# Layer 1's routed experts: the last tile of inner features, features 640 to 703 before, begins at feature 576 and spans 128

## The reference, cut to what matters

```python
def _L1_ffn_ref(x, gate_w, gate_b, w1, b1, w3, b3, w2, b2, sw1, sb1, sw3, sb3, sw2, sb2):
    ...
    scores = jax.nn.softmax(logits.astype(jnp.float32), axis=-1)
    top_vals, top_idx = jax.lax.top_k(scores, TOPK)
    ...
    h = jnp.einsum('td,edh->teh', xf, w1) + b1
    g = jnp.einsum('td,edh->teh', xf, w3) + b3
    a = jax.nn.silu(h) * g
    y = jnp.einsum('teh,ehd,te->td', a, w2, cw) + cw @ b2
    z = jax.nn.silu(xf @ sw1 + sb1) * (xf @ sw3 + sb3) @ sw2 + sb2
    return (y + z).reshape(shape)
```

## Time and profile before

| | us |
|---|---|
| median of 3 runs | 2023.27 (2022.45 to 2024.18) |
| the profiled execution, its own time | 2018.79 |
| its span, first to last instruction | 2017.1 |
| PE busy | 1900.9 (94%) |
| DVE busy | 691.0 (34%) |
| ACT busy | 561.0 (28%) |
| POOL busy | 201.3 (10%) |
| PE, weight loads | 1293.5 (64%) |

### The profile page before, as it was taken

How to read it: one execution, slowest core, us unless ns; L and a number is a source line. 1 busy time by engine, 2 the same in 40 slices (tenths; PEclk the granted TensorE clock), 3 DMA queues, 4 the chain that set the end, 5 groups by cost and what they waited for, 6 DMA issues and landing times.

```text
span 2017.1 us, 26698 instructions
## 1 busy us (share of the span) xinstructions
PE 1900.9 (94%) x10722; PEld 1293.5 (64%) x10722; DVE 691.0 (34%) x1706; ACT 561.0 (28%) x1263; POOL 201.3 (10%) x293
## 2 busy tenths in 40 slices
PE   5999999999999999998999978999898999999995
PEld 3677777777548447555777755777545544777773
DVE  4234344343335654421000145555425322111111
ACT  2333333332123224212222235444425200111110
POOL 0000000000010232322111031111001110000001
PEclk9999999999999998999999998999899999999998
DMA  5011111101320010027999730102212300877762
GB/s 194 22 42 43 37 69 43 42 22 64 125 104 1 21 42 30 36 83 259 352 354 352 277 119 32 48 32 90 105 42 84 149 22 16 318 289 285 284 252 80
DMA packets 43802, 245.19 MB, mean 122 GB/s; under 512 B 5929, under 2 KB 6433, under 8 KB 20880
## 3 DMA queue, kind: packets, MB, share of 16 engines
q1 hardware_dynamic: 30752, 213.22, 28.7%
q0 software_dynamic: 6000, 17.58, 2.7%
q10 hardware_dynamic: 6912, 12.52, 1.6%
HBM read 227.73 MB, written 15.57 MB: 121 GB/s over the span
## 4 chain that ended last, share of the span: by engine, by line
PE 86%; DVE 5%; issue 5%; DMA 2%; POOL 1%; ACT 1%; POOLq 0%; SPq 0%; DVEq 0%; ACTq 0%
PE bank L224 25%; PE bank L548 25%; PE bank L1606 10%; PE bank L230 8%; PE bank L690 3%; PE bank L718 2%; PE bank L2483 2%; PE bank L637 2%; PE bank L644 2%; PE bank L1186 2%; PE bank L1590 1%; PE bank L983 1%; PE bank L997 1%; PE bank L1211 1%; PE bank L975 1%
## 5 line engine op out<-in xcount | busy, mean ns | idle before, releaser
L548 PE MATMUL bank<-split 128*128 128x512 f32 x2208 | 549.1, 401 | 24.9 <-DVE split L521 12.3
L548 PEld LDWEIGHTS bank<-split 128*128 128x128 f32 x2208 | 407.3, 190 | 155.6 <-issue 31.6
L224 PEld LDWEIGHTS bank<-arena,weights 128*128 128x128 f32 x1984 | 229.7, 187 | 36.1 <-issue 33.7
L224 PE MATMUL bank<-xnT,weights 128*128 128x512 f32 (+1 forms) x592 | 246.7, 577 | 4.7 <-DVE xnT L880 3.1
L224 PE MATMUL bank<-arena,weights 128*128 128x128 f32 (+1 forms) x1984 | 245.1, 282 | 2.8 <-DVE arena L1597 1.8
L224 PEld LDWEIGHTS bank<-xnT,weights 128*128 128x128 f32 x592 | 113.2, 193 | 132.1 <-issue 124.8
L1606 PE MATMUL bank<-weights,arena 128*128 128x512 f32 (+1 forms) x368 | 166.6, 596 | 0.0
L230 PE MATMUL bank<-weights,arena 128*128 128x512 f32 x288 | 131.9, 611 | 8.3 <-ACT arena L2366 6.0
L1606 PEld LDWEIGHTS bank<-weights,arena 128*128 128x128 f32 (+1 forms) x368 | 65.9, 190 | 72.6 <-issue 72.6
L2593 DVE SCALAR_TENSOR_TENSOR arena<-bank,cols,arena 128x128 f32<-128x128 f32 x96 | 28.8, 345 | 230.7 <-PE bank L224 227.9
L230 PEld LDWEIGHTS bank<-weights,arena 128*128 128x128 f32 x288 | 54.8, 196 | 73.3 <-issue 62.9
(11 more groups left out here) (284 smaller groups left out, 2014.5 us busy)
## 6 DMA issues: line engine op xcount, KB each, us to landing
weights<-in_L_ffn_re_w SPq DMA_DIRECT2D x62, 1024.0 KB, 8.2
weights<-in_L_w SPq DMA_DIRECT2D x20, 1408.0 KB, 12.0
arena<-in_ctxT SPq DMA_DIRECT2D x24, 1024.0 KB, 5.0
arena<-in_L_w SPq DMA_DIRECT2D x12, 1408.0 KB, 7.6
weights<-in_L_w_full SPq DMA_DIRECT2D x10, 1280.0 KB, 9.5
expert_out<-arena ACTq DMA_DIRECT2D x47, 256.0 KB, 8.3
weights<-in_L_ffn_sw SPq DMA_DIRECT2D x9, 1024.0 KB, 5.0
arena<-in_L_w_full SPq DMA_DIRECT2D x6, 1280.0 KB, 9.8
```

Source lines behind the costliest of these rows:

```text
L224: s = pe.matmul(out, w[:, k, j0:j0 + m], rhs(k), start=(k == 0), stop=(k == KT - 1))
L548: s = pe.matmul(bank[:, :], still, moving, start=(n == 0), stop=(n == len(order) - 1))
```

## The change

The last of layer 1's six tiles takes features 576 to 703, that is 128 of them, instead of 640 to 703. Its first 64 features are those of the tile before it once more. They are kept out of the result: ACT and DVE compute only partitions 64 to 127 of that tile, and partitions 0 to 63 of it in the three `hid` buffers are set to zero once, by three memsets on DVE after the fence, for which PE waits (`hid_zero`). The part of `w2` for the last tile is 128 rows in memory instead of 64, and the bias columns are laid out to match on the host.

```diff
-LAST1 = INTER1 - (HT1 - 1) * P
+LAST1 = INTER1 - P
...
-            self.rows_of = [P] * (hidden_tiles - 1) + [last_rows]
+            self.first_of = [m * P for m in range(hidden_tiles - 1)] + [last_first]
+            self.own_of = [0] * (hidden_tiles - 1) + [(hidden_tiles - 1) * P - last_first]
...
-                r = self.rows_of[m]
-                s = pe.matmul(banks[6 + ex % 2][:, :], self.hid[ex % 2][0:r, m, :], w2.view[0:r, m, :], start=(m == 0),
+                s = pe.matmul(banks[6 + ex % 2][:, :], self.hid[ex % 2][:, m, :], w2.view[:, m, :], start=(m == 0),
...
-            sp.dma_start(buf[0:LAST1, full:full + DIM], A["L1_w2_last"][ex]).then_inc(landed, 16)
+            sp.dma_start(buf[:, full:full + DIM], A["L1_w2_last"][ex]).then_inc(landed, 16)
...
         stage_end(pe, "tensor")
+        pe.wait_ge(hid_zero, 3)
         moe1.turn_rows(pe, 0)
...
-                        r, o = moe1.rows_of[m], (m - m0) * P
-                        s = project_into(pe, banks[2 + 2 * n + j][0:r, o:o + P], w.view, m * P, r,
+                        o = (m - m0) * P
+                        s = project_into(pe, banks[2 + 2 * n + j][:, o:o + P], w.view, moe1.first_of[m], P,
...
         stage_end(dve, "vector")
+        for h in (*moe1.hid, moe1.hid_long):
+            dve.memset(h[0:moe1.own_of[HT1 - 1], HT1 - 1, :], 0.0).then_inc(hid_zero, 1)
         moe1.rows_vector(dve, 0)
...
-                dve.scalar_tensor_tensor(out=moe1.hid[ex % 2][0:r, m, :], in0=banks[3 + 2 * n][0:r, o:o + P],
-                                         scalar=col("b3", HT1 * ex + m, 1, 0, r),
-                                         in1=expert_silu[(HT1 * ex + m) % 3][0:r, 0:P], op0=ALU.add,
+                dve.scalar_tensor_tensor(out=moe1.hid[ex % 2][r:P, m, :], in0=banks[3 + 2 * n][r:P, o:o + P],
+                                         scalar=col("b3", HT1 * ex + m, 1, r, P),
+                                         in1=expert_silu[(HT1 * ex + m) % 3][r:P, 0:P], op0=ALU.add,
...
-    A["L1_w2_last"] = w[:, full:]
+    A["L1_w2_last"] = w[:, LAST1:]
```

More of the change, by code:

```diff
@@ L1361, in build_program, with __init__ @@
     class Experts:
-        def __init__(self, layer, n, chosen, hidden_tiles, last_rows, L, S, before=None):
+        def __init__(self, layer, n, chosen, hidden_tiles, last_first, L, S, before=None):
             self.layer, self.n, self.chosen, self.ht = layer, n, chosen, hidden_tiles
-            self.rows_of = [P] * (hidden_tiles - 1) + [last_rows]
+            self.first_of = [m * P for m in range(hidden_tiles - 1)] + [last_first]
+            self.own_of = [0] * (hidden_tiles - 1) + [(hidden_tiles - 1) * P - last_first]
             self.aff, self.top = S(NT, n), S(NT, 8)
@@ L1762, in rest_tensor @@
                     for n, w in enumerate(up):
[L1763 removed]
+                        s = project_into(pe, banks[2 + n][:, 0:3 * P], w, self.first_of[m], P, lambda k: self.tokT_long[:, k, :])
                     s.then_inc(r["mm"], 1)
@@ L1771, in rest_tensor @@
                     for m in range(self.ht):
-                        rows_ = self.rows_of[m]
-                        s = pe.matmul(banks[6][:, :], self.hid_long[0:rows_, m, c * P:(c + 1) * P], w2[0:rows_, m, :],
+                        s = pe.matmul(banks[6][:, :], self.hid_long[:, m, c * P:(c + 1) * P], w2[:, m, :],
                                       start=(m == 0), stop=(m == self.ht - 1))
@@ L1835, in build_program @@
     L(NT, DIM)
-    moe0 = Experts(0, E0, TOP0, HT0, P, L, small_layout())
+    moe0 = Experts(0, E0, TOP0, HT0, (HT0 - 1) * P, L, small_layout())
     sh_hid = Layout(L.at)(KT, TOK)
@@ L2406, in build_program @@
     sh1_mm, sh1_a, sh1_v, sh1_pool = sh_mm.then(22), sh_a.then(11), sh_v.then(11), sh_pool.then(NT)
-    sh1_down, sh1_add = sem("sh1_down"), sem("sh1_add")
+    sh1_down, sh1_add, hid_zero = sem("sh1_down"), sem("sh1_add"), sem("hid_zero")
     GROUPS = [[0, 1, 2, 3], [4, 5, 6, 7], [8, 9, 10]]
@@ L2587, in experts1_vector @@
                 n, j = divmod(m, 4)
-                r, o = moe1.rows_of[m], j * P
+                r, o = moe1.own_of[m], j * P
                 moe1.wait(dve, "silu", HT1 * ex + m + 1)
@@ L2600, in rest_hidden @@
         def rest_hidden(e, ex, m):
-            r = moe1.rows_of[m]
+            r = moe1.own_of[m]
             e.wait_ge(moe1.r["a"], moe1.hidden_a(ex, m))
-            return e.scalar_tensor_tensor(out=moe1.hid_long[0:r, m, :], in0=banks[3][0:r, 0:3 * P],
-                                          scalar=col("b3", HT1 * ex + m, 1, 0, r), in1=expert_silu[0][0:r, :],
+            return e.scalar_tensor_tensor(out=moe1.hid_long[r:P, m, :], in0=banks[3][r:P, 0:3 * P],
+                                          scalar=col("b3", HT1 * ex + m, 1, r, P), in1=expert_silu[0][r:P, :],
                                           op0=ALU.add, op1=ALU.mult)
@@ L2624, in experts1_scalar @@
                 n, j = divmod(m, 4)
-                r, o, at = moe1.rows_of[m], j * P, HT1 * ex + m
+                r, o, at = moe1.own_of[m], j * P, HT1 * ex + m
                 moe1.wait(act, "up_mm", 4 * ex + 2 * n + 1)
@@ L2628, in experts1_scalar @@
                     moe1.wait(act, "hid", at - 2)
-                act.activation(expert_silu[at % 3][0:r, 0:P], banks[2 + 2 * n][0:r, o:o + P], ACT.Silu,
-                               bias=col("b1", at, 1, 0, r)).then_inc(moe1.raised("silu"), 1)
+                act.activation(expert_silu[at % 3][r:P, 0:P], banks[2 + 2 * n][r:P, o:o + P], ACT.Silu,
+                               bias=col("b1", at, 1, r, P)).then_inc(moe1.raised("silu"), 1)
             if ex:
@@ L2640, in rest_silu @@
                 moe1.wait_hidden(e, ex - 1, HT1 - 1)
-            return e.activation(expert_silu[0][0:r, :], banks[2][0:r, 0:3 * P], ACT.Silu,
-                                bias=col("b1", HT1 * ex + m, 1, 0, r))
+            return e.activation(expert_silu[0][r:P, :], banks[2][r:P, 0:3 * P], ACT.Silu,
+                                bias=col("b1", HT1 * ex + m, 1, r, P))
         moe1.if_over(act, lambda e: moe1.rest_scalar(e, rest_silu))
@@ L2746, in column, with overlapped @@
         return v.reshape(-1, P).T
+    def overlapped(v):
+        return np.concatenate([v[:, 0:(HT1 - 1) * P], v[:, LAST1:]], 1)
     def rope_half(w, half):
@@ L2791, in lay_out @@
         "bq": column(I["L1_xattn_bq"]), "bk": column(I["L1_xattn_bk"]), "bv": column(I["L1_xattn_bv"]),
-        "b1": column(padded(I["L1_ffn_b1"], HT1 * P).reshape(-1)),
-        "b3": column(padded(I["L1_ffn_b3"], HT1 * P).reshape(-1)),
+        "b1": column(overlapped(I["L1_ffn_b1"]).reshape(-1)), "b3": column(overlapped(I["L1_ffn_b3"]).reshape(-1)),
         "sb1": column(I["L1_ffn_sb1"]), "sb3": column(I["L1_ffn_sb3"])}
```

1 line of the change is left out of this document (removed).

## The result

| | before | after |
|---|---|---|
| median | 2023.34 us (8 runs, 2019.14 to 2024.18) | 2008.31 us (8 runs, 2005.80 to 2015.10) |
| ratio, 95% interval | | 0.9932 (0.9918 to 0.9945) |
| the profiled execution's span | 2017.1 us | 2006.8 us |

The kernel is faster by 15.0 us in the medians. The ratio, 0.9932, by itself is 13.8 us, and its interval makes it 11 to 17 us.

A forecast was written before the change was run, and what follows sets the result against it. PE's own stream was taken as the bound. Savings of 12.9 + 0.9 + 0.7 + 1.2 = 15.7 us, less 1.0 for memsets and wait, take 14.7 off the 2023.27 median: 2008.6 us, range 2004 to 2013.

The forecast's parts named there:

- PE's stream alone sets the stage: Layer 1's expert stage: a microsecond taken from PE's stream comes off the end, one added on other engines is hidden.
- Removed, a period: Per expert in layer 1, priced by layer 0: 17.29 us becomes 16.30, 0.99 less; 13 periods give 12.9 us.
- The ends: Last period without transposes 16.80 to 15.87 us, 0.93 less; two final down projections 11.15 to 10.48, 0.67 less.
- Memsets and the wait: Behind the fence, three DVE memsets delay PE's first transpose by 1.0 us, bounds 0.4 to 1.4; a gain is excluded.
- Costed at nothing, ACT and DVE on other partitions: Last tile's 64x128 instructions move to other partitions at no cost, with over 190 us of waiting for PE as cover.
- Costed at nothing, the larger w2: w2's last part is 256 KB instead of 128, 4.87 MB an expert, hidden by about 11 us of cover.
- The sum: 15.7 us saved on PE less 1.0 for memsets and wait: 14.7 us less for the whole kernel.
- Run level: Profiled execution 2018.79 us becomes 2004.1; timed runs lie 4.5 higher, so the median 2023.27 becomes 2008.6.
- wide loads in line: Rival, layer 1 up projections: 256 wider weight loads at 56 ns give back 14.3 us, no gain, 2022.9 us; 3%.
- the partial removal: Rival: stalls at transposes and down-to-up borders stay, about 0.35 us a period; gain some 10 us, 2014; 3%.
- the DMA bound: Rival: 274 GB/s is all the stage can draw, 17.8 us an expert, slower at 2027.7 us; 2%.
- The rival of one half-clock piece more or less: PE after the fence: one half-clock stretch more gives 2010.2 us, one less 2007.0; 10% for one more.

The follow-up runs named there:

- both halves: The changed kernel with only the down projection wide, 2018.25 us (ratio 0.9981 to before), and with only the up projections wide, 2013.37 us (0.9961).
- narrow_grouped: The kernel before with its last four up tiles reordered so the two narrow ones stand together, same matmuls; 2016.24 us, ratio 0.9979.
- layer0_rows64: The changed kernel with 64 rows instead of 128 in the last inner tile of layer 0's down projections; 2019.03 us, ratio 0.9990 to the kernel before.
- zero_rows_w2: The changed kernel without memsets or PE's wait; ACT and DVE compute all 128 partitions, w2's doubled rows are zeros; 2005.06 us, again 2005.57.

## Why the prediction was right

Its forecast was 2008.6 us for a median of 2008.31. By its steps:

- **PE's stream alone sets the stage.** Right: in the steady stretch PE is busy for 211.00 of 211.00 us after as before, and both halves shortened the end by what they took from the stream.
- **Removed, a period.** Forecast 16.30 us; measured 16.306. Up 10.72 (10.71 forecast), transposes 0.43 (0.43), down 5.15 (5.16). Pricing by layer 0's identical code needed no theory of the stall at all. That it is the crossing, and not the narrow matmul or its load, was only argued then; `narrow_grouped` and `layer0_rows64` show it.
- **The ends.** The last period 15.87 (15.87), the last two down projections 10.47 (10.48).
- **Memsets and the wait.** Forecast 1.0 us, measured 0.90: three memsets in 0.71 us, not 0.95, and 0.19 until the first of them starts. The prediction excluded a gain; there is a small one, 1.51 us in place of 1.61 from the first transposes to the up projections behind them, so the net cost was 0.8. Why is open.
- **Costed at nothing, ACT and DVE on other partitions.** This step failed for one expert. 190 us of idle time hide it in general, but at expert 1 there is no down projection behind the transposes, and PE waits for DVE's copy. There up starts 1.92 us behind the transposes in place of 1.49 (1729.51 to 1731.00), 0.43 later. 0.09 of it are there in `zero_rows_w2` too (1.58): DVE's first product starts 0.27 us behind the transposes with all tiles wide, 0.18 before. Of the other 0.34, the upper partitions make up about 0.24 and the three memsets the rest. The cover was an average over the stage, while the prediction itself says that experts 0 and 1 have no down projection ahead of them.
- **Costed at nothing, the larger w2.** Right: PE waited for no weight.
- **The sum.** From the last `x_tok` addition to the end 15.9 us less, of which 1.6 are the clock of the first expert, leaves 14.3; forecast 14.7, less the 0.43 missed, and 0.2 back from the memsets, is 14.5. The forecast's parts hold one by one to within 0.2 us.
- **Run level.** That the changed kernel's profiled execution would be 2004.1 us was wrong by 4.4 (its own time 2008.53): the two profiled executions do not share a clock history. The step on the median, which took only the difference, held. That 2008.6 met 2008.31 this closely is partly chance, as the interval of 11 to 17 us says.

Of the rivals, wide loads in line fell by the period, the partial removal by the border from down to up (12 starts of down in 5.15 us are 0.43 each, the step into up included), the DMA bound by 300 GB/s at a share of 0.78, with PE busy throughout. The rival of one half-clock piece more or less did show in single executions, both ways: the first expert's up projections took 10.79 us in one execution of the changed kernel and 12.14 in another.

## What to carry to other kernels

Where most stationary operands fill the array and a few take only half its rows or columns, look at the distances between matmul starts on both sides of the few: here a crossing pair cost 0.3 to 0.4 us. The half tile saves next to nothing against that, since the moving operand is as wide as ever: the widened matmuls start 0.112 us apart in the changed kernel, and eight narrow ones, crossing included, took 1.02 us. Fill the tile up, by overlap with zeros in the weight, or at least put the narrow tiles side by side. A stage of the same kernel that runs the same code without the odd shape gives the price better than any model. And a cost is hidden only where its cover stands: check the first and the last iteration of a software pipeline on their own.

## What the runs showed of the hardware that I had not expected

- 96 rows or 96 columns cost no crossing (periods 7.45 and 7.43 us against 7.44), 64 of either do (7.84 and 7.72). So do 31 rows (3.62 us for eight matmuls in place of 3.44), but transposes with 16 stationary columns don't (0.43 us for four, as with 128).
- The pieces at half clock scatter by several microseconds between executions of the same instructions (4.6 us between two executions of the changed kernel, 1719.82 and 1715.27 us, up to the same addition). The kernel's times follow the mean granted clock: of its eight executions the two shortest, 2005.80 and 2005.90 us, had 0.975, the longest, 2015.10, had 0.969.
- DVE work on partitions 64 to 127 instead of 0 to 63 lengthened the stretch from the first of two products to the copy behind them from 0.52 to 0.78 us in the steady state, at equal shapes.
- A DVE memset of fp32 grew by 0.83 ns for each further column (165 ns for 128 columns, 1978 for 2304), while three in a row held PE up by 1.04 ns for each, gaps included.
